# A second output projection inside the experts' stage behind it, and one recurrence ahead of the last group's slots

## The chip, the cores and the metric

One Trainium2 chip, one of its cores. The time is that of one execution on the device, in microseconds (us), median of the runs. Lower is better.

## The reference

Four different layers follow each other on 4 batches of 1024 tokens with 128 features, each of the form x = x + s * silu(f), s from a token mixer and f from a feed-forward part, both on the layer-normed x. Only parts of the second and the third layer matter here, given in outline. `layernorm` without scale stands for `_layernorm`.

```python
# layer 1: attention, 16 heads of 8; its output projection
attn = jax.nn.softmax(energy, axis=-1) / sqrt(E)
out = jnp.einsum('bihv,bvhd->bihd', attn, v).reshape(B, N, E)
s = out @ W_out + b_out
# layer 1: feed-forward, each token through 2 of 8 experts
f = sum over the 2 chosen of  w * (gelu(xn @ W1[e] + b1[e]) @ W2[e] + b2[e])
f = layernorm(f) * gamma + beta
x = x + s * silu(f);  xn = layernorm(x)
# layer 2: a linear recurrence of complex powers A, written there with an FFT
y = real(ifft(fft(xn) * fft(C * A^t * B))) + D * xn
# layer 2: feed-forward, 2 of 8 experts with room for 640 tokens each
```

## The kernel before

Every stage is a `Stage` (L28): tensors of its own, semaphores, one block with a program for each engine, and at its end a barrier of all engines. SyncE issues nearly all loads and stores, in the order in which its program has them; GpSimd issues the sends of rows to places given by an index. All arithmetic is in f32 here. TOK is 4096, in 32 tiles of 128 tokens or 8 chunks of 512.

- `narrow_attention_stage` (L625) leaves in memory the unnormalised output `o1` [128 features, 4096] and the sums of the softmax `sums1` [16 heads, 4096]. Beside it the tokens' rows are sent to `sorted_x`, sorted by expert.
- `divided_projection` (L1206), a stage named "out": SyncE loads the sums as [128, 512] (L1224), the weights, the bias, and half of o in pieces (L1228). VectorE inverts the sums (L1265), SyncE stores the inverse (L1230), waits for it, and loads it spread over each head's 8 rows in eight chunks (L1234), with the rest of o between (L1236). VectorE divides a chunk (L1257), TensorE projects its four tiles into one of four banks (L1246), VectorE adds the bias and writes `s` (L1261).
- `sorted_experts_stage` (L1790), named "experts", runs 72 tiles of 128 sorted rows, four to a turn. For tile n: SyncE loads its rows (L1836, L1841) once tile n-4 is turned and its index kept; TensorE turns it (L1878, bank `xt`) and multiplies by its expert's first matrix (L1885, `up`), VectorE adds the bias (`add_bias`, L1955), ScalarE takes the gelu (L1934), TensorE turns the result (L1892) and multiplies it by the second matrix (L1901, `down`), VectorE adds that bias (`finish`, L1960), GpSimd weighs the rows (L1852) and sends them back to their tokens (L1855). TensorE's body for n is: turn n+2, up of n+1, turn the hidden rows of n, down of n-1. The first four bodies and the last four are written out, the rest is a loop (`iterations`, from L1822).
- `combine_and_send_stage` (L2393), named "mix1": for four groups of 8 tiles, sum of the two experts' rows, norm, gate, x, norm of x, turning into `xnT`, router scores (`score_group`, L2562), ranking, slots (`place_group`, L2590 to 2615), and GpSimd's 16 sends a group (L2498). VectorE's program runs them in an order written by hand, the scores and slots of group g-1 inside group g, and ends with `score_group(3)`, `rank_group(3)`, `place_group(3)` and then four recurrences `recur(b)` (L2617 to 2642), one per batch, each 8 instructions of 1024 columns. TensorE turns each result (L2700) and ScalarE copies it to `s` (L2760). The next stage is the experts' of layer 2.

Two lines set the ends that matter below:

```python
for b in range(BATCH):
    recur(b)                       # L2667, at VectorE's end
...
with eng.Fori(1, NL - 1) as j:     # L1825, the experts' loop
```

## Time and profile before

| | |
|---|---|
| median of 3 runs | 3506.58 us (3506.2 to 3508.32) |
| the profiled execution | 3507.76 us |
| its span, first to last instruction | 3506.0 us |
| TensorE busy, share of the span | 2860.7 us, 82% |
| VectorE | 2360.2 us, 67% |
| ScalarE | 1848.7 us, 53% |
| GpSimd | 1519.4 us, 43% |
| mean granted TensorE clock | 0.911 |
| transfers | 189.53 MB, mean 54 GB/s |

The shares are means over fifteen stages with different limits, so they are to be read stage by stage: the second output projection from 2592.3 to 2618.8, the experts of layer 1 from 2618.8 to 2841.7, mix1 from 2841.7 to 3029.8. In a timeline row stand the start in us from the span's start, the length, the engine (PE is TensorE, DVE VectorE, ACT ScalarE, POOL GpSimd, SPq SyncE's queue), the line, what is written and read, and in brackets the idle time before it with what ended it.

### The profile page before, as it was taken

What the parts mean: (1) busy time and instruction counts of PE and PEld (TensorE: products, weight loads), DVE (VectorE), ACT (ScalarE), POOL (GpSimd) and SP (SyncE); (2) the same over time, 40 slices, a digit from 0 to 9 for tenths busy, and PEclk for the clock granted to TensorE, in tenths of its full rate; (3) what the DMA queues carried; (4) which work ended last, traced back from release to release, by engine and by line L of the source; (5) the groups of instructions that cost most, each with busy time, mean ns of one, the idle gap of its engine ahead of it and who ended that gap; (6) DMA issues with size and microseconds to landing.
All of it is one profiled execution on the core that took longest, in us unless ns stands there. A gap on an engine that the chain in (4) does not pass through costs nothing. (4 is left out here: it accounts for less than half of the span.)

```text
span 3506.0 us, 66844 instructions
## 1 busy us (share of the span) xinstructions
PE 2860.7 (82%) x21143; PEld 1282.3 (37%) x21144; DVE 2360.2 (67%) x3457; ACT 1848.7 (53%) x2993; POOL 1519.4 (43%) x1115
## 2 busy tenths in 40 slices
PE   3999999999999996499965599999969932484994
PEld 1333333333333335433333122222226622362772
DVE  5666666666666655788886799999933346634663
ACT  2555555555555550144464399999954443244442
POOL 0889998999899991100000001101106625360000
PEclk9999999999999997799986699999989965696995
DMA  2011111111111114400003222222221150014001
GB/s 85 30 42 47 42 54 41 47 50 46 42 47 55 42 39 156 148 1 1 0 2 128 62 54 53 57 51 53 54 80 44 45 190 29 25 42 98 11 13 54
DMA packets 264612, 189.53 MB, mean 54 GB/s; under 512 B 148254, under 2 KB 210070, under 8 KB 263552
## 3 DMA queue, kind: packets, MB, share of 16 engines
q1 hardware_dynamic: 256288, 174.05, 17.5%
q0 software_dynamic: 8224, 14.24, 1.3%
q8 instruction: 50, 0.82, 0.1%
q14 instruction: 50, 0.41, 0.0%
HBM read 105.21 MB, written 67.55 MB: 49 GB/s over the span
## 5 line engine op out<-in xcount | busy, mean ns | idle before, releaser
L331 POOL TENSOR_TENSOR attn_esum<-attn_esum,attn_prob 128x1024 f32<-128x1024 f32 x384 | 904.4, 2355 | 30.8 <-ACT attn_prob L482 7.4
L553 DVE TENSOR_REDUCE attn_half_max<-attn_peek 128x2 f32<-128x1024 f32 x512 | 627.1, 1225 | 399.3 <-PE attn_peek L382 395.5
L482 ACT ACTIVATE attn_prob<-attn_score 128x1024 f32<-128x1024 f32 x512 | 512.8, 1022 | 247.3 <-PE attn_score L365 247.3
L848 ACT ACTIVATE attn_prob<-attn_score 128x512 f32<-128x512 f32 x1024 | 556.3, 596 | 72.5 <-PE attn_score L798 58.4
L865 DVE TENSOR_REDUCE attn_half_max<-attn_peek 128x2 f32<-128x1024 f32 x512 | 583.5, 1214 | 11.1 <-PE attn_peek L784 11.1
L412 PE MATMUL attn_acc<-attn_prob,attn_v 128*64 128x512 f32 x2048 | 487.9, 597 | 0.1
L814 PE MATMUL attn_acc<-attn_prob,attn_v 128*32 128x256 f32 x4096 | 327.8, 392 | 12.0 <-ACT attn_out L840 10.6
L1780 POOL DMA_INDIRECT sorted_x<-attn_sent_rows,attn_send x64 | 62.7, 980 | 555.1 <-PE attn_score L798 555.1
L784 PE MATMUL attn_peek<-attn_ke,attn_qe 48*128 48x512 bf16 x1024 | 203.0, 393 | 46.4 <-DMA attn_ke<-k 31.7
L382 PE MATMUL attn_peek<-attn_hi 64*128 64x512 f16 x1024 | 200.1, 388 | 34.4 <-DVE attn_half_max L553 34.4
L798 PE MATMUL attn_score<-attn_qe,attn_ke 49*128 49x512 bf16 x1024 | 200.6, 389 | 8.1 <-ACT attn_prob L848 6.0
L331 POOL TENSOR_TENSOR attn_esum<-attn_prob 128x1024 f32<-128x1024 f32 x64 | 151.0, 2360 | 126.7 <-ACT attn_prob L482 126.7
L412 PEld LDWEIGHTS attn_acc<-attn_prob,attn_v 128*64 128x64 f32 x2048 | 130.8, 137 | 201.1 <-issue 156.4
L1584 PE MATMUL experts_up<-experts_x,experts_up_w 128*128 (+1 forms) x816 | 200.0, 381 | 1.4 <-DVE experts_down_w L1673 1.4
L367 PE MATMUL attn_score<-attn_hi 64*128 64x512 f16 x1024 | 195.0, 378 | 0.0
L367 PE MATMUL attn_score<-attn_hi,attn_lo 64*128 64x512 f16 x1024 | 195.0, 377 | 0.0
L367 PE MATMUL attn_score<-attn_lo,attn_hi 64*128 64x512 f16 x1024 | 195.0, 377 | 0.0
L365 PE MATMUL attn_score<-attn_shift,attn_sel 64*128 64x512 bf16 x1024 | 194.8, 377 | 0.0
L1955 DVE TENSOR_TENSOR experts_pre<-experts_up,experts_b 128x512 f32<-128x512 f32 x112 | 77.4, 691 | 147.0 <-PE experts_up L1885 147.0
L2052 POOL MEMSET proj_zero<- 128x2340 f32 x1 | 2.0, 2048 | 381.6 <-POOLq L41 381.6
L1650 ACT ACTIVATE experts_a<-experts_up 128x512 f32<-128x512 f32 x136 | 81.2, 597 | 159.1 <-PE experts_up L1584 156.1
L1940 ACT ACTIVATE experts_hidT<-experts_ht 128x512 f32<-128x512 f32 x112 | 66.9, 597 | 165.0 <-PE experts_ht L1892 165.0
(516 smaller groups left out, 4603.6 us busy)
## 6 DMA issues: line engine op xcount, KB each, us to landing
attn_xb<-attn_x_all SPq DMA_DIRECT2D x66, 256.0 KB, 2.5
attn_invB<-inv SPq DMA_DIRECT2D x64, 256.0 KB
o<-attn_out SPq DMA_DIRECT2D x32, 512.0 KB, 2.7
out_o<-o SPq DMA_DIRECT2D x8, 2048.0 KB
mix_f<-picked SPq DMA_DIRECT2D x16, 512.0 KB, 7.4
experts_x<-sorted_x SPq DMA_DIRECT2D x112, 65.0 KB
attn_qe<-q SPq DMA_DIRECT2D x192, 32.0 KB
attn_ke<-k SPq DMA_DIRECT2D x192, 32.0 KB
```

The costliest lines, as they stand in the source:

```text
L331: nc.gpsimd.tensor_tensor(own, before, prob[:, u % NPROB, :, :], ALU.add).then_inc(added, 1)
L367: last = mm(score[:, u % 2, h, :], ks[r, slot, WHICH["k"], keys], qs[r, slot, WHICH["q"], queries], start=(n == 0), stop=False)
L382: last = mm(peek[:, h, :], hi[r, slot, WHICH["q"], t * P:(t + 1) * P], hi[r, slot, WHICH["k"], half * CH:(half + 1) * CH], start=True, sto ...
L412: last = mm(acc[rows_of(h), :], v[:, slot, t, rows_of(h)], prob[:, u % NPROB, h, :], start=(t == 0), stop=(t == KT - 1))
L482: nc.scalar.activation(prob[:, u % NPROB, :, :], score[:, u % 2, :, :], ACT.Exp).then_inc(exped, 1)
L553: V.tensor_reduce(half_max[:, half, :, t], peek[:], AX.X, ALU.max, negate=True).then_inc(maxed, 1)
L784: last = mm(peek[:, m % NPEEK, n, :], qe[r, slot, pair, t * P:(t + 1) * P], ke[r, slot, pair, half * CH:(half + 1) * CH], start=True, stop ...
L798: last = mm(score[:, (PAIR * k + n) % RING, :], ke[r, slot, pair, t * P:(t + 1) * P], qe[r, slot, pair, c * CH:(c + 1) * CH], start=True, ...
L814: last = mm(acc[h * COL:(h + 1) * COL, cols], v[:, slot, t, h, :], prob[:, (HG * s + h) % NPROB, cols], start=(t == 0 and p == 0), stop=(t ...
L848: nc.scalar.activation(prob[:, n % NPROB, :], score[:, n % RING, :], ACT.Exp).then_inc(exped, 1)
L865: V.tensor_reduce(half_max[:, half, PAIR * pair:PAIR * (pair + 1), t], peek[:, m % NPEEK, :, :], AX.X, ALU.max, negate=True).then_inc(maxe ...
L1584: ins = nc.tensor.matmul(out, ws[pw][:, cols], xs[px][own], start=start and n == 0, stop=stop and n == 2)
```

## The change

1. The stage "out" is gone. What it did is a class `DividedProjection`, which `sorted_experts_stage` takes as `beside` for layer 1 (not for layer 2). Its loads stand in SyncE's queue behind those of the first four tiles; o comes in one load. The store of the inverse and its eight loads stand behind the load of tile 7. VectorE inverts and scales behind its first body, and divides one chunk behind each of the bodies 4 to 11.
2. For that, two more turns (bodies 4 to 11) are written out instead of being in the loop, on TensorE, VectorE and SyncE. Behind body 11 TensorE projects all 32 tiles in eight rounds of four into the two banks of `xt`, VectorE takes each round, and TensorE goes on when the last is taken.
3. In mix1 `recur(0)` stands ahead of the scores, ranks and slots of the last group; each recurrence waits for its own group's rows in `xnT` and the first no longer for all four.

```diff
-def divided_projection(nc, name, o_d, sums_d, inv_d, scale, w, bias, s):
...
 
-def sorted_experts_stage(nc, name, ident, blocks, xs_d, expert_d, weights, y_d):
+class DividedProjection:
+
+
+
+    AT = 4
+    ROUNDS = NT // AT
+
+    def __init__(self, st, nc, o_d, sums_d, inv_d, scale, w, bias, s):
+        self.nc, self.o_d, self.sums_d, self.inv_d, self.scale, self.w, self.bias, self.s = nc, o_d, sums_d, inv_d, scale, w, bias, s
+        self.heads = sums_d.shape[0]
+        assert TOK == P // self.heads * CH
+        self.o, self.inv, self.sums = st.sb("attn_o", [P, TOK]), st.sb("attn_inv", [P, NCH, CH]), st.sb("attn_sums", [P, CH])
+        self.wt, self.bias_b = st.sb("attn_wt", [P, D]), st.sb("attn_bias", [P, D])
+        self.w_in, self.sums_in, self.inv_out, self.o_in, self.inverted, self.scaled, self.divided, self.projected, self.summed = (
+            st.sem(n) for n in ("w_in", "sums_in", "inv_out", "o_in", "inverted", "scaled", "divided", "proj_done", "proj_summed"))
+        self.inv_in = [st.sem(f"inv_in{n}") for n in range(NCH)]
+
+    def pieces(self, a):
+        return a.rearrange("h (n t) -> (h n) t", n=P // self.heads)
+
+    def tiles(self, r):
+        return range(r * self.AT, (r + 1) * self.AT)
+
+    def load(self, sp):
+        sp.dma_start(self.sums[:], self.pieces(self.sums_d)).then_inc(self.sums_in, DMA)
+        sp.dma_start(self.wt[:], self.w).then_inc(self.w_in, DMA)
+        sp.dma_start(self.bias_b[:], broadcast_rows(self.bias)).then_inc(self.w_in, DMA)
+        sp.dma_start(self.o[:], self.o_d[:]).then_inc(self.o_in, DMA)
+
+    def spread(self, sp):
+        sp.wait_ge(self.inverted, 1)
+        sp.dma_start(self.pieces(self.inv_d), self.sums[:]).then_inc(self.inv_out, DMA)
+        sp.wait_ge(self.inv_out, DMA)
+        for i in range(NCH):
+            sp.dma_start(self.inv[:, i, :], self.inv_d[:, i * CH:(i + 1) * CH].unsqueeze(1).to_broadcast([self.heads, P // self.heads, CH])
+                         ).then_inc(self.inv_in[i], DMA)
+
+    def invert(self, dve):
+        V = self.nc.vector
+        dve.wait_ge(self.sums_in, DMA)
+        V.reciprocal(self.sums[:], self.sums[:]).then_inc(self.inverted, 1)
+        dve.wait_ge(self.w_in, 2 * DMA)
+        V.tensor_scalar(self.wt[:], self.wt[:], self.scale, None, ALU.mult).then_inc(self.scaled, 1)
+
+    def divide(self, dve, i):
+        dve.wait_ge(self.o_in, DMA)
+        dve.wait_ge(self.inv_in[i], DMA)
+        own = slice(i * CH, (i + 1) * CH)
+        self.nc.vector.tensor_tensor(self.o[:, own], self.o[:, own], self.inv[:, i, :], ALU.mult).then_inc(self.divided, 1)
+
+    def project(self, pe, bank, r):
+        if r == 0:
+            pe.wait_ge(self.scaled, 1)
+            pe.wait_ge(self.divided, NCH)
+        if r >= 2:
+            pe.wait_ge(self.summed, r - 1)
+        for n, t in enumerate(self.tiles(r)):
+            last = self.nc.tensor.matmul(bank[:, n * P:(n + 1) * P], self.o[:, t * P:(t + 1) * P], self.wt[:], start=True, stop=True)
+        last.then_inc(self.projected, 1)
+
+    def take(self, dve, bank, r):
+        dve.wait_ge(self.projected, r + 1)
+        own = self.tiles(r)
+        self.nc.vector.tensor_tensor(self.s[:, own[0]:own[-1] + 1, :], bank[:].rearrange("p (t d) -> p t d", d=D),
+                                     self.bias_b[:].unsqueeze(1).to_broadcast([P, len(own), D]), ALU.add).then_inc(self.summed, 1)
+
+
+def sorted_experts_stage(nc, name, ident, blocks, xs_d, expert_d, weights, y_d, beside=None):
...
         names = ("consts", "x_turned", "x_copied", "projected", "biased", "gelu_done", "h_turned", "h_copied", "summed", "y_ready")
         (consts, x_turned, x_copied, projected, biased, gelu_done, h_turned, h_copied, summed, y_ready) = (st.sem(n) for n in names)
         stored, kept, shared, loaded = st.sem("stored"), st.sem("kept"), st.sem("shared"), [st.sem(f"loaded{u}") for u in range(UNROLL)]
+        job = beside(st) if beside else None
         block = st.block()
         NCONST = 2
 
-        def iterations(eng, body):
+        def iterations(eng, body, between=None):
             for u in range(UNROLL):
                 body(u, u, True, False)
-            with eng.Fori(1, NL - 1) as j:
+            START = 3 if between else 1
+            for n in range(1, START):
+                for u in range(UNROLL):
+                    body(UNROLL * n + u, u, False, False)
+            if between:
+                between()
+            with eng.Fori(START, NL - 1) as j:
                 for u in range(UNROLL):
                     body(UNROLL * j + u, u, False, False)
             for u in range(UNROLL):
...
             sp.dma_start(b2[:], broadcast_rows(weights.weights_d[3].rearrange("e d -> (e d)"))).then_inc(consts, DMA)
             for n in range(UNROLL):
                 sp.dma_start(x[:, n, :], xs_d[n * P:(n + 1) * P, :]).then_inc(loaded[n], DMA)
-            with sp.Fori(1, NL) as l:
+            AHEAD = 3 if job else 1
+            if job:
+                job.load(sp)
+            for l in range(1, AHEAD):
+                for u in range(UNROLL):
+                    sp.wait_ge(x_turned, UNROLL * (l - 1) + u + 1)
+                    sp.wait_ge(kept, UNROLL * (l - 1) + u + 1)
+                    sp.dma_start(x[:, u, :], xs_d[(UNROLL * l + u) * P:(UNROLL * l + u + 1) * P, :]).then_inc(loaded[u], DMA)
+                if l == 1:
+                    job.spread(sp)
+            with sp.Fori(AHEAD, NL) as l:
                 for u in range(UNROLL):
                     sp.wait_ge(x_turned, UNROLL * (l - 1) + u + 1)
                     sp.wait_ge(kept, UNROLL * (l - 1) + u + 1)
...
             turn_x(0, 0, False)
             turn_x(1, 1, False)
             project(0, 0, False)
-            iterations(pe, body)
+
+            def attention():
+                pe.wait_ge(x_copied, 3 * UNROLL + 2)
+                for n in range(job.ROUNDS):
+                    job.project(pe, xt[:, n % 2, :], n)
+                pe.wait_ge(job.summed, job.ROUNDS)
+
+            iterations(pe, body, attention if job else None)
             down(blocks - 1, 1, True)
 
         @block.scalar
...
 
             dve.wait_ge(consts, NCONST * DMA)
             add_bias(0, 0, False)
-            iterations(dve, body)
+
+            def with_division(n, u, first, final):
+                body(n, u, first, final)
+                if isinstance(n, int) and n == 0:
+                    job.invert(dve)
+                elif isinstance(n, int) and 4 <= n < 4 + NCH:
+                    job.divide(dve, n - 4)
+
+            def attention():
+                for n in range(job.ROUNDS):
+                    job.take(dve, xt[:, n % 2, :], n)
+
+            if job:
+                iterations(dve, with_division, attention)
+            else:
+                iterations(dve, body)
             finish(blocks - 1, 1)
 
...
             def recur(b):
                 u = xnT[:, b * SEQ:(b + 1) * SEQ]
                 Er, Ei, Wr, Wi, decay = (kept[:, n, :] for n in range(KEPT))
+                dve.wait_ge(evacuated, b + 1)
                 if b == 0:
-                    dve.wait_ge(evacuated, NG)
                     dve.wait_ge(kept_in[0], DMA)
                 link(V.tensor_tensor(vr, Er, u, ALU.mult))
                 if b == 0:
...
                 second_factors(g)
                 if g:
                     place_group(g - 1)
+            recur(0)
             score_group(NG - 1)
             rank_group(NG - 1)
             place_group(NG - 1)
-            for b in range(BATCH):
+            for b in range(1, BATCH):
                 recur(b)
 
         @block.tensor
...
             weights = ExpertWeights(held, nc, "experts1", inputs("L1_ffn_", "W1 b1 W2 b2"))
             narrow_attention_stage(nc, ident, q1, k1, v1, o1, sums1, scratch("max1", [2, 2, 16, P], BF16),
                                    lambda st: RowScatter(st, s, send, pick_weight, sorted_x, weights, picked[1]))
-            divided_projection(nc, "out1", o1, sums1, scratch("inv1", [16, TOK]), D ** -0.5, a["L1_attn_W_out"], a["L1_attn_b_out"], s)
-            sorted_experts(1, BLOCKS, weights)
+            inv1 = scratch("inv1", [16, TOK])
+            sorted_experts(1, BLOCKS, weights, lambda st: DividedProjection(st, nc, o1, sums1, inv1, D ** -0.5, a["L1_attn_W_out"],
+                                                                            a["L1_attn_b_out"], s))
         ROOM = 5 * TOK // 4 // P
         with ExitStack() as held:
             weights = ExpertWeights(held, nc, "experts2", inputs("L2_ffn_", "w1 b1 w2 b2"))
```

SyncE, from the end of attention, before (`out_` is the projection's stage, `inv` and `o` lie in memory):

```order
L1224 DMA out_sums<-sums 128x512
L1225 DMA out_wt<-in_L_attn_W_out 128x128
L1226 DMA out_bias_b<-in_L_attn_b_out 128x128
L1228 DMA out_o<-o 128x512 x4
L1230 DMA inv<-out_sums 128x512
L1234 DMA out_inv<-inv 128x1x512 x5
L1236 DMA out_o<-o 128x512
L1234 DMA out_inv<-inv 128x1x512
L1236 DMA out_o<-o 128x512
L1234 DMA out_inv<-inv 128x1x512
L1236 DMA out_o<-o 128x512
L1234 DMA out_inv<-inv 128x1x512
```

and with the change (`attn_` in the experts' stage is the projection's):

```order
L1837 DMA experts_expert<-owner 1x72
L1838 DMA experts_b<-in_L_ffn_b 128x1024
L1840 DMA experts_x<-sorted_x 128x130 x4
L1744 DMA experts_attn_sums<-sums 128x512
L1745 DMA experts_attn_wt<-in_L_attn_W_out 128x128
L1746 DMA experts_attn_bias<-in_L_attn_b_out 128x128
L1747 DMA experts_attn_o<-o 128x4096
L1848 DMA experts_x<-sorted_x 128x130 x4
L1751 DMA inv<-experts_attn_sums 128x512
L1754 DMA experts_attn_inv<-inv 128x1x512 x8
L1848 DMA experts_x<-sorted_x 128x130 x4
```

The four tiles that stood behind a stage's end now stand ahead of the projection's loads, and tiles 4 to 7 and 8 to 11 behind its two bundles.

TensorE in the experts' stage, with the change, end of body 11 and the loop's first turn:

```order
L1915 MATMUL experts_out<-experts_w,experts_hidT 128x128
L1915 ISA
L1915 MATMUL experts_out<-experts_w,experts_hidT 128x128
L1777 MATMUL experts_xt<-experts_attn_wt,experts_attn_o 128x128 x32
L1829 UNCONDITIONAL_BRANCH
L1829 ISA
L1891 REGISTER_ALU
L1892 MATMUL experts_xt<-identity,experts_x 128x128
L1881 ISA
L1881 TENSOR_LOAD experts_expert
```

Before, the 32 products stood alone in their stage (L1246) and the loop began behind body 3.

VectorE in mix1, at the end of the third group's slots, before:

```order
L2614 TENSOR_TENSOR mix_each_pick<-mix_hot,mix_weight 128x128
L2615 TENSOR_REDUCE mix_sent_rows<-mix_each_pick 128x2x8
L2562 TENSOR_TENSOR mix_score<-mix_lg,mix_bias_b 128x64
L2563 TENSOR_REDUCE mix_red<-mix_score 128x8
L2564 TENSOR_TENSOR mix_shifted<-mix_score,mix_red 128x64
L2573 TENSOR_REDUCE mix_red<-mix_score 128x8
```

and with the change:

```order
L2650 TENSOR_TENSOR mix_each_pick<-mix_hot,mix_weight 128x128
L2651 TENSOR_REDUCE mix_sent_rows<-mix_each_pick 128x2x8
L2659 TENSOR_TENSOR mix_f<-mix_kept,xnT 128x1024
L2662 TENSOR_TENSOR mix_f<-mix_kept,xnT 128x1024
L2665 SCALAR_TENSOR_TENSOR mix_f<-mix_kept,mix_f 128x1024
L2666 SCALAR_TENSOR_TENSOR mix_f<-mix_kept,mix_f 128x1024
L2669 TENSOR_TENSOR mix_f<-mix_f,mix_kept 128x1024
L2672 TENSOR_TENSOR mix_f<-mix_f,mix_kept 128x1024
L2673 TENSOR_TENSOR mix_f<-mix_f 128x1024
L2678 SCALAR_TENSOR_TENSOR mix_f<-xnT,mix_dd,mix_f 128x1024
L2598 TENSOR_TENSOR mix_score<-mix_lg,mix_bias_b 128x64
L2599 TENSOR_REDUCE mix_red<-mix_score 128x8
```

Eight instructions of 1024 columns have moved ahead of the last group's scores; the other three recurrences stay at the end.

## Rows read from the trace of the kernel before

**Rows 1.** Windows by stage: engine busy us (count), TensorE clock, DMA share, GB/s.
```profile
2592.30:2618.80 26.50, 11.16 (x64) 10.24 (x64) 13.76 (x18) 0.00 (x0) 0.00 (x0) 0.65 0.65 184
2618.80:2841.70 222.90, 186.95 (x1080) 130.38 (x1080) 70.77 (x144) 94.19 (x218) 131.33 (x217) 0.97 0.16 43
2841.70:3029.80 188.10, 34.47 (x144) 30.21 (x144) 133.79 (x340) 59.54 (x104) 71.56 (x77) 0.50 0.31 99
```

**Rows 2.** Timeline of the second output projection: start us, us, engine, line [idle before].
```profile
2592.34 0.36 SPq L1224 DMA_DIRECT2D out_sums<-sums  x1
...
2595.02 3.35 DVE L1265 RECIPROCAL out_sums<-out_sums 128x512 f32<-128x512 f32 x1 [34.10 <-DMA out_sums<-sums]
2598.29 0.16 DVE L1267 TENSOR_SCALAR out_wt<-out_wt 128x128 f32<-128x128 f32 x1
2598.40 0.33 SPq L1230 DMA_DIRECT2D inv<-out_sums  x1
2600.64 3.18 SPq L1234 DMA_DIRECT2D out_inv<-inv  x5
...
2604.58 0.69 DVE L1257 TENSOR_TENSOR out_o<-out_o,out_inv 128x512 f32<-128x512 f32 x1 [6.12 <-DMA out_inv<-inv]
```

**Rows 3.** DMA view of window 2602.5 to 2613.5.
```profile
DMA packets 1615, 2.96 MB, mean 269 GB/s; under 512 B 175, under 2 KB 175, under 8 KB 1614
```

**Rows 4.** Timeline, first us of the experts' stage.
```profile
2618.78 0.25 SPq L1833 DMA_DIRECT2D experts_expert<-owner  x1
...
2628.58 0.69 DVE L1955 TENSOR_TENSOR experts_pre<-experts_up,experts_b 128x512 f32<-128x512 f32 x1 [1.06 <-PE experts_up L1885]
...
2630.52 0.69 DVE L1955 TENSOR_TENSOR experts_pre<-experts_up,experts_b 128x512 f32<-128x512 f32 x1 [1.25 <-PE experts_up L1885]
...
2631.85 0.27 PE L1878 MATMUL experts_xt<-identity,experts_x 128*128 128x128 f32 x1
```

**Rows 5.** Timeline of mix1 from the third group's slots to the next stage.
```profile
2948.16 0.29 DVE L2615 TENSOR_REDUCE mix_sent_rows<-mix_each_pick 128x16 f32<-128x128 f32 x1
...
2948.96 3.58 PE L2684 MATMUL mix_lg<-mix_wr,xnT 128*128 128x8 f32 x16 [1.11 <-ACT xnT L2735]
...
2962.96 0.23 DVE L2562 TENSOR_TENSOR mix_score<-mix_lg,mix_bias_b 128x64 f32<-128x64 f32 x1 [14.52 <-DMA o<-attn_out]
...
2976.73 1.21 DVE L2623 TENSOR_TENSOR mix_f<-mix_kept,xnT 128x1024 f32<-128x1024 f32 x1
...
2988.98 1.23 DVE L2623 TENSOR_TENSOR mix_f<-mix_kept,xnT 128x1024 f32<-128x1024 f32 x1
...
3001.11 0.98 POOL L2498 DMA_INDIRECT sorted_x<-mix_sent_rows,mix_send  x1 [0.30 <-issue]
...
3029.78 0.26 SPq L1833 DMA_DIRECT2D experts_expert<-owner  x1
```

**Rows 6.** Timeline, last loop tiles of the experts' stage, VectorE.
```profile
2819.52 0.69 DVE L1955 TENSOR_TENSOR experts_pre<-experts_up,experts_b 128x512 f32<-128x512 f32 x1 [0.98 <-PE experts_up L1885]
...
2820.85 0.29 DVE L1960 TENSOR_TENSOR experts_y<-experts_out,experts_b 128x128 f32<-128x128 f32 x1 [0.64 <-PE experts_out L1901]
...
2821.96 0.69 DVE L1955 TENSOR_TENSOR experts_pre<-experts_up,experts_b 128x512 f32<-128x512 f32 x1 [0.82 <-PE experts_up L1885]
```

**Rows 7.** Timeline, projection products at the lower and at the full clock.
```profile
2605.42 6.53 PE L1246 MATMUL out_acc<-out_wt,out_o 128*128 128x128 f32 x32 [18.22 <-DVE out_o L1257]
...
2614.85 2.36 PE L1246 MATMUL out_acc<-out_wt,out_o 128*128 128x128 f32 x16 [0.18 <-DVE out_o L1257]
```

**Rows 8.** Timeline, first and fifth of five up-projections, TensorE.
```profile
2629.25 1.12 PE L1885 MATMUL experts_up<-experts_w,experts_xT 128*128 x2 [0.25 <-issue]
...
2640.60 1.12 PE L1885 MATMUL experts_up<-experts_w,experts_xT 128*128 x2 [0.23 <-issue]
```

**Rows 9.** Windows of the experts' stage, split where the granted clock changes.
```profile
2621.30:2628.10 6.80, 4.15 (x7) 1.59 (x7) 0.69 (x1) 2.32 (x5) 0.73 (x4) 0.50 0.33 91
2628.10:2832.00 203.90, 182.80 (x1074) 128.79 (x1073) 70.08 (x143) 91.84 (x214) 129.56 (x211) 1.00 0.16 43
```

63 lines of the change are left out of this document (2 added, 61 removed).

## The prediction

> **What bounds the kernel now.** One core runs stage after stage with a barrier between them, so a microsecond counts only where it shortens the chain of its own stage. The busy shares of the page are means over such stages, and its chain of waits ends in the very last stage; neither says anything of the two places that change. I read the windows of the two stages, then their timelines in order of time, then the transfers.
>
> In the second output projection, window 2592.3 to 2618.8, TensorE works 11.2 us of 26.5 and ScalarE and GpSimd nothing [rows 1]. Its timeline is one chain [rows 2]: the sums' load is issued at 2592.34, VectorE inverts them at 2595.02 for 3.35 us, the inverse goes out to memory at 2598.40 and comes back spread over the heads from 2600.64 on, the first division stands at 2604.58. Behind it the loads of o and of the inverse run at 269 GB/s, full [rows 3]. The stage costs latency and transfer, not arithmetic. It ends where the experts' first load is issued, 2618.78 [rows 4].
>
> The experts' stage behind it, 222.9 us for 72 tiles, has TensorE busy 187 us and VectorE 71 us [rows 1]: TensorE sets its pace and VectorE has room. In mix1 (the combination, the routing and the recurrences) VectorE is the chain: 133.8 of 188.1 us busy. Its longest idle time there is 14.52 us, from 2948.45 to 2962.96, ahead of the last group's scores [rows 5]. The name beside that wait is a transfer of an early stage, which cannot be it. By the program VectorE waits for TensorE's score products, and these are shown from 2948.96 for 3.58 us, so over at 2952.54: 4.1 us of the wait are explained, 10.4 us are not. The runs of before lie within 2.1 us of each other, so I take those 10.4 us as present in all of them.
>
> **The change, part by part.** Times after a "+" count from the experts' first load, 2618.78 before.
>
> *The stage of its own goes.* From 2592.34 to 2618.78: -26.4 us. The barrier between attention and whatever follows stays.
>
> *The experts' first loads.* SyncE now issues sums, weights, bias and o between the first four tiles and tiles 4 to 7, and they share the transfers' bandwidth. In front of tile 4 lie 0.51 MB of biases, 0.26 of tiles, 0.39 of sums, weights and bias and 2.10 of o, 3.3 MB together; at 269 GB/s [rows 3] that is 12.2 us, from about +2: tile 4 lands near +15. It was turned at 2631.85, +13.1 [rows 4]: 2 us late. The Trainium skill (DMA: Bandwidth & Descriptors, section Queues, rings and completion order) says that each DMA engine consumes descriptors in the order of its ring, which is what would put tile 4 behind o; no row here shows the order, and without it tile 4 would be in time and the next term would stand alone.
>
> *VectorE's inversion*, 3.35 us, and the scaling of the weights, 0.16 [rows 2], stand between the second and the third addition of the up-projection's bias. These are at 2628.58 (0.69 long) and 2630.52 [rows 4], with 1.25 us between them: the third comes 2.3 us late, and the activation, TensorE's turning and the output behind it as well. This runs beside the late tile 4; the larger counts: +2.4 us. At the mean rate of the old stage, 184 GB/s [rows 1], tile 4 would land at +20 and this term be 7.
>
> *SyncE's queue.* Behind tile 7 it waits for the inverse (+14), stores it, waits for the landing (2.24 us between the two issues at 2598.40 and 2600.64 [rows 2]) and issues eight loads of 0.64 us (3.18 for five): free for tile 8 at +22. The 2.1 MB of the inverse take 7.8 us from +17, so tile 8 lands near +26; with a pace of 2.83 us tile 8 is wanted at +15.3 + 4 x 2.8 = +26.5. I take +0.3 us; between 0 and 4 by the slower rate.
>
> *Eight divisions*, 0.69 us each, one behind each of tiles 4 to 11. At the quickest pace seen VectorE's output addition ends at 2821.14 and the next bias addition begins at 2821.96 [rows 6]: 0.82 us, enough. Cost 0, cover: VectorE's wait for TensorE. Without it 8 x 0.69 = 5.5.
>
> *The projection itself* stops TensorE between tiles 11 and 12, and with it all who wait for it. Ahead: VectorE's last output addition and last division, 0.29 + 0.69, and two hand-overs, 1.2 us. Then eight rounds of four products: 16 rows (two rounds) took 2.36 us [rows 7], 1.18 a round, 9.4 together; VectorE's addition of 0.69 per round fits under it with two banks. Behind: the last addition and hand-overs, 0.9. Sum 11.5 us, against 10.0 if what ScalarE does meanwhile saves a bubble at the restart, and 15.2 at the lower clock, where 32 rows took 6.53 us (most of them at half clock), 1.63 a round [rows 7].
>
> *Eight bodies written out* in place of two turns of the loop. The first four, also written out, took 2640.60 - 2629.25 = 11.35 us from one up-projection to the fourth behind it [rows 8], the whole stage from 2628.1 to 2832.0 at 2.83 us a tile (203.9 us for 72, [rows 9]): no gain from straight code at this end of the stage, so 0. At the far end 2.44 us a tile are seen (2819.52 to 2821.96, [rows 6]); that would be 8 x 0.39 = -3.1. The Trainium skill (Runtime: NRT & Kernel Launch, section Instruction fetch mechanics) says that a taken branch breaks the sequential prefetch and straight code hides it; by that alone the sum would be 3.1 us lower, and the first four bodies speak against it here.
>
> *The first batch's recurrence ahead of the last group's slots.* One recurrence takes VectorE 2988.98 - 2976.73 = 12.25 us [rows 5]. It needs only the first two groups' rows (already turned) and buffers that are free by then. In its new place it fills 2948.45 to 2960.7 and the scores still start when the signal comes, 2962.96: -12.25 us at VectorE's end, which sets the stage's: only the last turning and its copy follow it, and the next stage begins at 3029.78 [rows 5]. Queued behind it: GpSimd's sends of the last group, which ended at 3002.1 [rows 5] and move by at most a microsecond or two, while VectorE will end near 3013. Bounds: -4.1 if the unexplained 10.4 us start anew behind the recurrence, -14.5 if they vanish.
>
> **Sum.** -26.4 + 2.4 + 0.3 + 11.5 = -12.2 for the projection, -12.25 for the recurrence: -24.5. The profiled execution took 3507.76 us, its span 3506.0; that gives 3483.3, and the median of the three runs lies 1.2 below the profiled one: **3482 us**. A measurement of this kernel can tell about 0.2%, 7 us, from no change.
>
> **Rivals.**
> 1. *Tiles starve.* The 4.2 MB of o and inverse share the way with tiles that come just in time. For: the arrival times above are late, or early by half a microsecond. Against: 269 GB/s held for 11 us. At 184 GB/s: + 4.5 + 2.5, **3489**. Chance 0.15.
> 2. *The late signal moves along.* If whatever holds TensorE's score signal for 10.4 us starts only where VectorE has nothing to do, it comes behind the recurrence and only 4.1 us are gained: **3490**. For: nothing explains it. Against: GpSimd's sends run beside it either way. 0.12.
> 3. *Better than the sum.* The signal comes at once (-2.3) and the written-out bodies keep the pace of the far end (-3.1): **3477**. For: both numbers stand in rows; against: the first four bodies. 0.18. The Trainium skill's rule on branches, cited above, is its second half.
> 4. *TensorE stays at the lower clock in the experts' stage.* At full clock it is the pace. The stage spends 2621.3 to 2628.1 at half clock after idle time of TensorE, then 204 us at full [rows 9]; the change makes the first 15 us of the stage thinner. If the clock fell for the stage, each tile would cost 1.63/1.18 of 2.83 us, 1.08 more, 72 x 1.08 = 78 us: **3560**. It decides from 24.5 / 1.08 = 23 tiles at half clock on. Against: after the old stage's longer idle time it rose 7 us into the work. 0.03. The Trainium skill (TensorE: Matmul & The Clock Gate, HAM oscillation) says that idle stretches of TensorE bring the lower clock back, which is the mechanism of this rival.
> 5. *The new chain does nothing for the end*: the gains of both parts are eaten by waits that I don't see. 3505; 0.02.
>
> **How the numbers follow.** The forecast, 3478 to 3487, has 0.50. Rivals 1 and 2 reach 3490, with the uncovered divisions 3496; rival 3 and the refill bubble reach 3474. Range 3473 to 3496; it leaves out rivals 4 and 5 and mixtures. Faster by over 0.2% (below 3499.6) are the forecast and rivals 1 to 3: 0.95. Rival 5: same, 0.02. Rival 4: slower, 0.03.
>
> **What would show it.** The experts' first load near 2592.3. The reciprocal right behind the second bias addition; the third near +14.1. The turning of tile 4 at +15, of tile 8 at +26.5, with a wait for a transfer under 1 us. The divisions without a shift of the next bias addition. A gap of 11.5 us in TensorE's expert work with 64 rows in it. The experts' stage 236 to 238 us long. In mix1 the first recurrence at once behind the third group's slots, then under 3 us of idle time, mix1 12 us shorter. Wrong would be: waits for tiles of 4 us and more (rival 1), a wait of 10 us behind the recurrence (rival 2), half clock beyond the first 10 us of the experts (rival 4).

## The result and the profile after

| | before | after |
|---|---|---|
| median | 3506.39 us (3503.86 to 3508.32, 4 runs) | 3478.78 us (3475.54 to 3481.29, 4 runs) |
| ratio, 95% interval | | 0.9921 (0.9904 to 0.9938) |
| profiled execution, its span | 3507.76, 3506.0 | 3476.27, 3474.6 |
| second output projection and experts' stage | 26.4 + 222.9 | 235.6 |
| mix1 | 188.1 | 172.6 |

The change takes 27.6 us off; 24.5 were forecast. Windows by stage of the kernel after, in the order of [rows 1] (TensorE, its weight loads, VectorE, ScalarE, GpSimd, then granted clock, DMA share, GB/s):

```profile
2590.90:2826.50 235.60, 196.67 (x1144) 139.05 (x1144) 84.25 (x162) 94.52 (x218) 131.63 (x217) 0.96 0.22 62
2826.50:2999.10 172.60, 34.23 (x144) 30.14 (x144) 133.94 (x340) 59.54 (x104) 73.69 (x77) 0.50 0.34 108
```

The first window is 12.7 us longer than its counterpart in [rows 1], and the window of 26.4 us ahead of it is gone: -13.7, where -12.2 was forecast. In mix1 VectorE has the same 340 instructions and the same 134 us of work, in 15.5 us less time; -12.25 was forecast. The two sum to -29.2, the profiled executions differ by 31.5; the rest lies in stages that the change doesn't touch (the experts' first load is issued 1.4 us earlier in the span than the old stage's was).

Timeline of the kernel after at the start of the experts' stage, whose first load is issued at 2590.91; the rows answer to [rows 4]:

```profile
2600.42 0.69 DVE L1976 TENSOR_TENSOR experts_pre<-experts_up,experts_b 128x512 f32<-128x512 f32 x1 [0.93 <-PE experts_up L1899]
...
2601.03 3.34 DVE L1760 RECIPROCAL experts_attn_sums<-experts_attn_sums 128x512 f32<-128x512 f32 x1
...
2604.36 0.68 DVE L1976 TENSOR_TENSOR experts_pre<-experts_up,experts_b 128x512 f32<-128x512 f32 x1
...
2605.72 0.33 PE L1892 MATMUL experts_xt<-identity,experts_x 128*128 128x128 f32 x1 [1.74 <-DMA experts_x<-sorted_x]
...
2606.57 2.01 PE L1899 MATMUL experts_up<-experts_w,experts_xT 128*128 x2 [0.52 <-ACT experts_xT L1948]
```

and the window of the clock's fall:

```profile
2606.70:2610.10 3.40, 3.40 (x11) 2.26 (x12) 0.69 (x1) 0.64 (x2) 1.24 (x2) 0.50 0.45 106
```

Tile 4 is turned at +14.8, as forecast (+15), and the third addition stands at +13.5 (forecast +14.1). What wasn't forecast is the last row: TensorE has just waited 1.74 us, its granted clock falls to 0.5 from 2606.7 to 2610.1, and the up-projection takes 2.01 us instead of 1.12. Tile 5 is turned at +19.6, 3.8 us later than before, not 2.4. By tile 13 only 2.1 of these are left (+40.56 against +38.44).

The same timeline at the insertion:

```profile
2634.51 0.68 DVE L1768 TENSOR_TENSOR experts_attn_o<-experts_attn_o,experts_attn_inv 128x512 f32<-128x512 f32 x1
2635.34 7.85 PE L1777 MATMUL experts_xt<-experts_attn_wt,experts_attn_o 128*128 128x128 f32 x64 [1.18 <-DVE experts_attn_o L1768]
2636.51 0.69 DVE L1783 TENSOR_TENSOR s<-experts_xt,experts_attn_bias 128x512 f32<-128x512 f32 x1 [1.31 <-PE experts_xt L1777]
...
2643.22 0.69 DVE L1783 TENSOR_TENSOR s<-experts_xt,experts_attn_bias 128x512 f32<-128x512 f32 x1 [0.20 <-PE experts_xt L1777]
2644.35 0.33 PE L1892 MATMUL experts_xt<-identity,experts_x 128*128 128x128 f32 x1 [1.16 <-DVE s L1783]
```

Lead 1.18 and end 1.16 us are near the forecast (1.2 and 0.9); the 64 rows take 7.85 us, 0.98 a round, not the 1.18 of [rows 7].

VectorE in mix1, from the third group's slots to the last group's scores and its slots, answering to [rows 5]:

```profile
2933.58 0.29 DVE L2651 TENSOR_REDUCE mix_sent_rows<-mix_each_pick 128x16 f32<-128x128 f32 x1
2933.78 1.21 DVE L2659 TENSOR_TENSOR mix_f<-mix_kept,xnT 128x1024 f32<-128x1024 f32 x1
...
2944.72 1.28 DVE L2678 SCALAR_TENSOR_TENSOR mix_f<-xnT,mix_dd,mix_f 128x1024 f32<-128x1024 f32 x1
2946.04 0.22 DVE L2598 TENSOR_TENSOR mix_score<-mix_lg,mix_bias_b 128x64 f32<-128x64 f32 x1
...
2952.94 0.28 DVE L2628 TENSOR_TENSOR_SCAN mix_upto<-mix_goes_on,mix_tally 128x64 f32<-128x64 f32 x1 [0.80 <-PE mix_tally L2728]
```

The 14.52 us of idle time are gone altogether, 2.3 more than the recurrence's 12.25. TensorE's score products ended at 2937.96 and their signal arrived at 2940.70, still 2.7 us late, but nobody waited for it. (This arrival is the semaphore's own record in the trace, which no row above shows; where VectorE waits, the start of the scores shows it too.)

### The profile page after: what moved, and what is told of

It is laid out like the page before. It is cut to its first block and busy times, and to the rows that moved or that the text cites. A ratio compares the mean times of both kernels' runs of the same rounds, so it can differ in the third digit from the quotient of the medians.

```text
span 3474.6 us, 66734 instructions
## 1 busy us (share of the span) xinstructions
PE 2857.3 (82%) x21143; PEld 1279.6 (37%) x21144; DVE 2359.7 (68%) x3457; ACT 1848.8 (53%) x2993; POOL 1521.8 (44%) x1115
## 3 DMA queue, kind: packets, MB, share of 16 engines
q1 hardware_dynamic: 255280, 174.05, 17.6%
## 5 line engine op out<-in xcount | busy, mean ns | idle before, releaser
L367 PE MATMUL attn_score<-attn_lo,attn_hi 64*128 64x512 f16 x1024 | 194.7, 377 | 0.0
L367 PE MATMUL attn_score<-attn_hi,attn_lo 64*128 64x512 f16 x1024 | 194.7, 377 | 0.0
L365 PE MATMUL attn_score<-attn_shift,attn_sel 64*128 64x512 bf16 x1024 | 194.7, 377 | 0.0
```

The source lines that it names most:

```text
L367: last = mm(score[:, u % 2, h, :], ks[r, slot, WHICH["k"], keys], qs[r, slot, WHICH["q"], queries], start=(n == 0), stop=False)
```

## The experiments

Each set of runs was made on one chip, with the kernel before run beside it there. The sets lie on different chips, and the kernel before had another median on nearly each: 3515.1, 3516.2, 3497.7 and 3497.8 us. So gains are compared within a set, and the lengths of stages are read from the profiles. A gain in us is worked out from the ratio; the difference of the two medians can be up to 3 us off it, since the sets are small.

### The parts, and what they cost

**The recurrence's move alone** (the kernel before, with `recur(0)` and its waits as in the diff of the change).

> Kernel before with the recurrence move alone. Theory: the two unexplained delays of TensorE's score signal (10.4 us in the kernel before, 2.7 us seen in the kernel after, hidden there) cost nothing once VectorE has work, so the routing stage gains the recurrence's 12.25 us, the rest of the idle time (14.5 - 12.25 = 2.3) and about 1.2 at the count behind it: 15.7 us, 3490.7. Rival (what the forecast said): the signal comes when it did, 12.25 us, 3494.2. Second rival: the delay starts anew behind the recurrence, 4.1 us, 3502.3. In the profile: no idle time of VectorE ahead of the last scores for the theory, 2.3 us for the first rival, 10 us for the second.

3495.57 us against 3515.05 (17 runs): ratio 0.9944 (0.9932 to 0.9956), 19.7 us. Mix1 takes 172.0 us, and VectorE has no idle time ahead of the last scores:

```profile
2963.24 1.28 DVE L2642 SCALAR_TENSOR_TENSOR mix_f<-xnT,mix_dd,mix_f 128x1024 f32<-128x1024 f32 x1
2964.56 0.22 DVE L2562 TENSOR_TENSOR mix_score<-mix_lg,mix_bias_b 128x64 f32<-128x64 f32 x1
```

Both rivals fall. The time is not the theory's 3490.7, which started from the first chip's 3506.4. The gain is 4 us above the theory's 15.7, just inside the interval (15.5 to 23.9 us); the runs below give a reason.

**The projection's part alone**, with the recurrences back at the end:

```diff
-            recur(0)
             score_group(NG - 1)
             rank_group(NG - 1)
             place_group(NG - 1)
-            for b in range(1, BATCH):
+            for b in range(BATCH):
                 recur(b)
```

> Kernel after with the recurrence put back behind the last group's slots. Theory: the projection's part gives the stage of its own (26.4) against 12.7 us more in the experts' stage: -13.7 from the two profiles, 3492.7; the forecast's sum for this part was -12.2, 3494.2. If the parts add up, this and the run with the recurrence alone together give 27.6. The wait of VectorE ahead of the last scores: 14.5 us if the late signal belongs to the program, another number if it belongs to one execution.

3500.61 us on the same chip: ratio 0.9960 (0.9947 to 0.9973), 14.1 us. The experts' stage is 236.3 us long: 13.0 us against the first profile, 14.1 against the run above on this chip, where the two stages take 27.4 and 223.0 us. The parts together give 33.8 on this chip, not 27.6. And mix1 takes 195.3 us, 7.2 more than before. Timeline around the last scores:

```profile
2957.51 0.98 POOL L2534 DMA_INDIRECT sorted_x<-mix_sent_rows,mix_send  x1 [0.30 <-issue]
2960.63 0.23 DVE L2598 TENSOR_TENSOR mix_score<-mix_lg,mix_bias_b 128x64 f32<-128x64 f32 x1 [23.19 <-DMA experts_attn_inv<-inv]
```

The wait is 23.19 us here, not 14.5. The products ended at 2941.53, so the signal is 19.1 us late. The transfer named as releaser is again no possible one; what can be read is the length. The send in the first row is the last of its group, and the signal comes 2.1 us behind its end.

**Without the 32 products and the eight additions.**

```diff
-            iterations(pe, body, attention if job else None)
+            iterations(pe, body, (lambda: None) if job else None)
...
-                iterations(dve, with_division, attention)
+                iterations(dve, with_division, lambda: None)
```

> Kernel after without the 32 products of the output projection and the eight additions that take them (their part of the result is left out; loads, inversion and divisions stay). Theory: the insertion costs what tile 14's turning moved less what the two other terms took, 10.3 us: 3468.5. Rival: the forecast's 11.5, 3467.3 (not to be told apart by the time alone, but by the turning of tile 14: +43.1 against +41.9). Second rival: ScalarE and VectorE use the pause and catch up, 5 us or less: 3474 or more.

3470.72 us. Tile 14 is turned 2.6 us behind tile 13; in the kernel after it was 12.9. The insertion costs 10.3 us, as the theory said. But the stage is only 7.1 us shorter (228.5) and the whole takes 3470.7 where the theory had 3468.5, since tile 13 is turned at +44.0, not +40.6:

```profile
2618.55 2.91 SPq L1848 DMA_DIRECT2D experts_x<-sorted_x  x2
2618.76 1.06 PE L1915 MATMUL experts_out<-experts_w,experts_hidT 128*128 x8
2623.60 0.33 PE L1892 MATMUL experts_xt<-identity,experts_x 128*128 128x128 f32 x1 [3.79 <-DMA experts_x<-sorted_x]
```

In this timeline (first load at 2594.22) tile 4 came with a wait of 0.86 us only and the clock did not fall behind it; TensorE wanted tile 8 at +25.6 and got it at +29.4. The kernel after, kept back at half clock behind tile 4, turned tile 8 at +27.3 without a wait. Tile 8 is where the forecast's first rival sat: it is a matter of 2 us, and here its wait, 3.79 us, is all but the 4 us that the rival named as its sign. Tile 5 is turned at +17.8 here, 2.0 us later than before; so nearly all of the way on to the kernel after's +19.6 is its half clock.

**Eight bodies written out, in the kernel before, and nothing else.**

```diff
+            for n in range(1, START):
+                for u in range(UNROLL):
+                    body(UNROLL * n + u, u, False, False)
-            with eng.Fori(1, NL - 1) as j:
+            with eng.Fori(START, NL - 1) as j:
```

> Kernel before with eight more bodies of the first experts' stage written out in place of two turns of the loop, nothing else. Theory: straight code runs a tile in 2.52 us against 2.83 in the loop, 8 x 0.31 = 2.5 us: 3503.9. Rival (the forecast): no difference, 3506.4; the 2.52 us of the kernel after would then come from something else there. In the profile: the distance of the up-projections of tiles 4 to 11. The routing stage is that of the kernel before: VectorE's wait ahead of the last scores is 14.5 us again if the late signal belongs to the program.

Ratio 0.9990 (0.9981 to 0.9999), 3.5 us; the experts' stage 220.85 us against 222.89. TensorE's up-projections, first of the kernel before (loop), then of this one:

```profile
2646.15 1.12 PE L1885 MATMUL experts_up<-experts_w,experts_xT 128*128 x2
2649.38 1.12 PE L1885 MATMUL experts_up<-experts_w,experts_xT 128*128 x2 [0.67 <-ACT experts_xT L1927]
2652.07 1.12 PE L1885 MATMUL experts_up<-experts_w,experts_xT 128*128 x2
```

```profile
2643.58 1.12 PE L1893 MATMUL experts_up<-experts_w,experts_xT 128*128 x2
2645.99 1.12 PE L1893 MATMUL experts_up<-experts_w,experts_xT 128*128 x2
2648.60 1.12 PE L1893 MATMUL experts_up<-experts_w,experts_xT 128*128 x2
```

In the loop the distance from one tile to the next is 3.2 us once in each turn, just behind the branch; in the part that is written out none is above 2.8 us. Two turns gave 2.0 us. Mix1 takes 193.4 us and VectorE's wait 21.7: the late signal again, 17.6 us behind the products' end at 2948.32:

```profile
2965.94 0.23 DVE L2570 TENSOR_TENSOR mix_score<-mix_lg,mix_bias_b 128x64 f32<-128x64 f32 x1 [21.72 <-DMA o<-attn_out]
```

### The late signal

**GpSimd's sends held back** (the kernel before):

```diff
                 pool.wait_ge(maps_ready, g + 1)
+                if g == NG - 2:
+                    pool.wait_ge(logits, NG)
```

> Kernel before, and GpSimd begins the third group's sends only when TensorE's score signal of the last group is there (it can hold them, since the last group's sends begin 8 us later than these end). In three profiles without the recurrence move this signal came 10.4, 17.6 and 19.1 us after the end of the last score product, while GpSimd sent without a pause. Theory: these sends hold the signal; without them it comes within 0.1 us, VectorE's wait falls to about 4.1 us, and the routing stage takes 188.1 - 10.4 = about 178 us, 10 to 17 us less than before. Rival: the sends have nothing to do with it (TensorE's own last product is reported late when it has nothing behind it): the wait stays at 14 to 23 us, the time that of before.

3500.21 us against 3516.23: ratio 0.9955 (0.9940 to 0.9970), 15.8 us, from one wait of GpSimd. Mix1 takes 176.5 us. Timeline; the products start at 2952.20 and end at 2955.78:

```profile
2952.20 3.58 PE L2686 MATMUL mix_lg<-mix_wr,xnT 128*128 128x8 f32 x16 [1.11 <-issue]
...
2955.82 0.23 DVE L2564 TENSOR_TENSOR mix_score<-mix_lg,mix_bias_b 128x64 f32<-128x64 f32 x1 [4.13 <-PE mix_lg L2686]
...
2956.63 0.98 POOL L2500 DMA_INDIRECT sorted_x<-mix_sent_rows,mix_send  x1 [4.87 <-issue]
```

The scores begin 0.04 us behind the last product, and the releaser is now named rightly. The sends begin behind it.

**The score products done twice**, on the same chip:

```diff
                 last.then_inc(logits, 1)
...
+                if g == NG - 1:
+                    for t in range(GT):
+                        mm(lg[:, 1 - g % 2, t * E:(t + 1) * E], xnT[:, (g * GT + t) * P:(g * GT + t + 1) * P], wr[:], start=True, stop=True)
```

> Kernel before, and TensorE does the last group's eight score products a second time, into the other bank, behind the signal. Theory (sends hold the signal): no change, VectorE's wait 14 to 23 us. Rival (a last product is reported late because nothing follows it on TensorE): the products behind it push it out, the wait falls to about 4.1 us and the routing stage to about 178 us.

Ratio 1.0001 (0.9991 to 1.0010). VectorE's wait is 22.50 us. TensorE goes on at once, and still the signal of the first 16 rows comes 18.4 us late:

```profile
2947.14 3.58 PE L2684 MATMUL mix_lg<-mix_wr,xnT 128*128 128x8 f32 x16 [1.11 <-issue]
2950.57 3.56 PE L2690 MATMUL mix_lg<-mix_wr,xnT 128*128 128x8 f32 x16
```

```profile
2969.12 0.23 DVE L2562 TENSOR_TENSOR mix_score<-mix_lg,mix_bias_b 128x64 f32<-128x64 f32 x1 [22.50 <-DMA o<-attn_out]
```

**The kernel after once more**, on another chip.

> The kernel after itself, unchanged, beside many runs of the kernel before. In the runs made so far with other kernels the kernel before had a median of 3515 to 3516 us, not 3506, and the late score signal took 17 to 19 us in three profiles against 10.4 in the first. Theory: the signal's lateness differs from execution to execution and the kernel after is rid of it, so its own time stays (3476 to 3481) while its gain is larger than the 27.6 us first measured: 35 us, ratio about 0.990. Rival: the whole chip was slower by 10 us in those runs, the ratio is 0.992 again and the kernel after takes about 3488.

3481.04 us against 3497.68: ratio 0.9960 (0.9946 to 0.9973), 14.0 us. The theory's first half holds: the kernel after takes its 3480 on this chip too (in the profile the score signal is 0.01 us behind the products). Its second half and the rival fall: the gain is not larger but half as large (the medians alone differ by 16.6), because the kernel before is faster here. That led to the last run.

**The kernel before once more**, on a further chip.

> The kernel before itself, profiled once more. Its median was 3506.4, 3515.1, 3516.2 and 3497.7 us in four sets of runs, on as many chips, while the kernel after took 3478.8 and 3481.0. Theory: the sets differ by the lateness of the score signal alone: the first profile has 3507.8 us with 10.4, so the whole is 3497.4 plus the lateness, within 3 us, in this profile too, whatever the chip; the routing stage is 177.7 us plus the lateness. Rival: the chips differ by their general pace: the lateness is 10.4 again and other stages (the experts' 222.9 us, the part behind it 476.3) take the difference.

The profiled execution took 3498.39 us. Timeline around the last scores:

```profile
2952.70 3.58 PE L2684 MATMUL mix_lg<-mix_wr,xnT 128*128 128x8 f32 x16 [1.11 <-ACT xnT L2735]
...
2956.32 0.22 DVE L2562 TENSOR_TENSOR mix_score<-mix_lg,mix_bias_b 128x64 f32<-128x64 f32 x1 [4.12 <-PE mix_lg L2684]
```

No lateness at all, with the same instructions and 16 sends beside them, and a time of 3497.4 + 0, within 1 us: the theory. The medians bear it out: 3515.1, 3516.2 and the first chip's 3506.4, less the 17.6, 18.4 and 10.4 us read there, give 3497.5, 3497.8 and 3496.0. For a single execution it holds less well: of two other profiles close to the kernel before, products twice (3512.6 us) less its lateness gives 3494.2, and bodies written out (3507.4 us) gives 3489.8 where some 3495 were to be expected, so other stages differ by 3 to 6 us as well. In one table:

| profile | score signal late by | mix1 | mix1 less lateness |
|---|---|---|---|
| before, first chip | 10.4 us | 188.1 | 177.7 |
| projection's part alone | 19.1 | 195.3 | 176.2 |
| bodies written out | 17.6 | 193.4 | 175.8 |
| products twice | 18.4 | 194.7 | 176.3 |
| sends held back | 0.0 | 176.5 | 176.5 |
| before, last chip | 0.0 | 176.3 | 176.3 |
| recurrence's move alone | 3.0, hidden | 172.0 | |
| after; after once more | 2.7, hidden; 0.0 | 172.6; 172.3 | |

The signal's lateness goes by the chip, as far as one or two profiles of each can tell: on the three chips where it is late without the move, five profiles with the move have it 2.7 to 3.0 us late; on the chip of the kernel after's second set three profiles with the move have 0.0. There the kernel before has no profile; its median, 3497.7 us, is that of the last chip. Without the move mix1 takes 176 us plus the lateness (the first row's other 1.6 us are a second late signal, behind its count), and with it 171.9 to 173.1 in eight profiles, whatever the chip. The move is worth 4 us by itself and all the lateness that a chip has. With the 13 to 14 us of the projection's part that makes 17 to 18 us on a chip without lateness; 14.0 were measured there, with an interval of 9.4 to 18.9.

### What is to be had beyond the change

**Another order of loads**: o behind tiles 4 to 7, tiles 8 and 9 between the inverse's store and its spread (the kernel after).

```diff
     def load(self, sp):
...
-        sp.dma_start(self.o[:], self.o_d[:]).then_inc(self.o_in, DMA)
-    def spread(self, sp):
+    def spread(self, sp, tile):
+        sp.dma_start(self.o[:], self.o_d[:]).then_inc(self.o_in, DMA)
...
+        tile(2, 0)
+        tile(2, 1)
         sp.wait_ge(self.inv_out, DMA)
```

> Kernel after with SyncE's loads in another order: o goes behind tiles 4 to 7 instead of ahead of them, and tiles 8 and 9 are issued between the inverse's store and its spread. Theory: tile 4 is turned at +13.1 again, not +14.8, TensorE does not fall to half clock behind it, and tile 8 is in time: 1.5 to 3 us less than the kernel after in the experts' stage (232.6 to 234), whole 0.1% less. Rival: o and the inverse come later, VectorE waits for a division and the insertion begins later: equal or slower.

3480.05 us, the experts' stage 236.5 us (0.9 more than after, with a fall to half clock for 3.4 us behind the insertion): no gain, though tile 4 is turned at +13.4 and tile 8 at +24.7, as the theory said. The rival's wait is there:

```profile
2622.28 0.69 DVE L1770 TENSOR_TENSOR experts_attn_o<-experts_attn_o,experts_attn_inv 128x512 f32<-128x512 f32 x1 [2.04 <-DMA experts_attn_inv<-inv]
```

Tile 13 is turned at +40.3, where the kernel after has it at +40.6. The 2 us only changed places.

**All bodies written out**, of both experts' stages and with SyncE's loads likewise, once with that order of loads and once with the order of the kernel after:

```diff
-            with eng.Fori(START, NL - 1) as j:
+            for n in range(1, NL - 1):
+                if n == 3 and between:
+                    between()
                 for u in range(UNROLL):
-                    body(UNROLL * j + u, u, False, False)
+                    body(UNROLL * n + u, u, False, False)
```

> The same order of loads, and every body of both experts' stages written out instead of a loop. Theory: the loop costs 0.3 us a tile (2.82 in the loop against 2.52 written out); 56 tiles of the first and 32 of the second stage are in the loop, 17 + 9.6 us, so some 26 us less than the run with the order of loads alone, about 3450. Rival: the 2.52 us hold only near the stage's start, where GpSimd's sends are not yet dense, and the pace of the later tiles is set elsewhere: no gain beyond 3 us. Second rival: so long a straight program starves the engines of instructions: slower.

> Kernel after with every body of both experts' stages written out, the loads in the order of the kernel after. Theory: straight code is all of the gain of the run with everything written out (14.3 us in the first, 7.4 in the second experts' stage), the order of the loads none of it: the experts' stages 221 to 223 us and 7 us shorter, the whole 21 us below the kernel after, about 3458. Rival: tile 8 is missed by 2 to 4 us as in the run without the products, 3461.

3459.01 us (ratio 0.9836, 0.9822 to 0.9849, against 3516.23) and 3458.42 us (0.9892, 0.9877 to 0.9907, against 3497.68). Each lies 21 to 23 us below the run of its own set that still has the loop (3480.05 and 3481.04). The first experts' stage takes 222.2 and 223.4 us, 12.3 to 14.3 less, the part behind mix1 6.5 to 7.4 less. Windows of 100 us inside the first experts' stage, of the kernel after and of the first of these runs:

```profile
2690.00:2790.00 100.00, 90.57 (x528) 63.47 (x529) 34.65 (x71) 45.10 (x107) 64.79 (x108) 1.00 0.17 46
```

```profile
2690.00:2790.00 100.00, 98.71 (x580) 69.46 (x579) 37.98 (x78) 49.20 (x116) 69.84 (x117) 1.00 0.19 51
```

TensorE goes from 91 to 99% busy: 580 rows against 528. At 15 rows a tile that is 2.59 us a tile instead of 2.84. In this stretch the stage is now bound by TensorE's work alone; its start and the insertion are not.

**Divisions and insertion later**, in the run with everything written out and the other order of loads: `n - 6` in place of `n - 4` in `with_division`, `n == 4` in place of `n == 3` above, and TensorE's wait for `x_copied` ahead of the insertion four tiles later.

> The run with everything written out and the other order of loads, and now the divisions stand behind tiles 6 to 13 instead of 4 to 11 and the insertion four tiles later. In that run VectorE waited 2.0 us for the first piece of the inverse, and the tiles 8 to 10 took 4.4 and 3.5 us instead of 2.6. Theory: the wait goes, the tiles up to the insertion keep 2.6 us, the first experts' stage is 2 to 3 us shorter (219 to 220), 3456. Rival: what is late next is a tile's load behind the eight pieces of the inverse; the same 222.

3457.09 us, the first experts' stage 221.9: the rival. VectorE's wait for the inverse is gone, and tile 10, whose load stands behind the eight pieces of the inverse, is late by 2.68 us instead. All three versions with everything written out are equal within what can be told.

## Why the prediction was right, and where it was not

- **The stage of its own, -26.4**: right for the first profile. In the five others that have the stage it took 26.7 to 28.9 us, so this term is good to some 2.5 us only.
- **The late tile 4, +2.4**: the mechanism was right, and tile 4 came at +14.8. The term was too small: behind the wait of 1.74 us the granted clock was at the lower level for 3.4 us, and tile 5 was 3.8 us late. The forecast had weighed the lower clock for the whole stage (rival 4) and not for one wait.
- **SyncE's queue, +0.3**: right in the kernel after, but by luck of 2 us. The load of tile 8 was issued at +21.9 as forecast (+22), but landed near +29.4 and not +26 in the run without the products; tile 8 waited for it there, and the kernel after was slow enough not to.
- **Eight divisions, 0**: right; none moved a bias addition.
- **The insertion, +11.5**: 10.3, since a round took 0.98 us and not the 1.18 of [rows 7]; the second of the rounds there had begun only when VectorE's division was done.
- **Written-out bodies, 0**: this step was wrong. "The first four bodies speak against it" read the wrong rows: the distance in [rows 8] ends in the loop already, three of its five up-projections (tiles 2, 3 and 4) are written out and two are not. Two turns written out gave 2.0 us, two thirds of rival 3's second half. The runs with everything written out give 0.25 us a tile, 1 us a turn of four tiles. The Trainium skill (Runtime: NRT & Kernel Launch, section Instruction fetch mechanics) has straight code faster because a taken branch breaks the sequential prefetch; the traces agree with the direction. They do not show the prefetch apart from the rest that a loop needs, its register arithmetic above all.
- **Sum of the projection's part**: +3.8, +10.3 and -1.7 (written-out bodies) give 12.4 where 12.7 were measured and 14.2 forecast. Three sizes were off, in both directions.
- **The recurrence, -12.25**: 15.5 in the profiles. The step that failed is "the scores still start when the signal comes", with a signal fixed at 14.5 us behind VectorE's last work. The delay isn't a fixed time: it was gone when GpSimd's sends were held back, and with VectorE at work 2.7 to 3.0 us of it were left. And "I take those 10.4 us as present in all of them" held for the first set of runs only: on the last chip it was 0, on another its time says the same, and on two it was 17.6 to 19.1. Of the gain in the first set 4 us are the plain wait filled, the rest the lateness. So that the whole gain came near the forecast is luck of the chip: on one without lateness the same change gave 14.0 us, and on one with more of it its two parts gave 33.8, where 24.5 were forecast. The time of the kernel after, 3479 to 3481 us, does not depend on it.
- **The rivals.** Rival 1 (tiles starve) did not come in the kernel after: tile 4 came when forecast and tile 8 was in time; the 1.4 us beyond the forecast behind tile 4 are the lower clock's. Rival 2 (the late signal moves along) is refuted: the scores follow the recurrence at once in each profile with the move. Rival 3 came true in both halves (3.2 where it had 2.3 us, though the signal did not come at once but was late out of sight; 2.0 where it had 3.1); the time of 3478.8 lies between its 3477 and the forecast's 3482. Rival 4 showed itself for 3.4 us only; its price for a tile at the lower clock, 1.63/1.18 = 1.38 times as long, was too low, since the same up-projection took 2.01 us there against 1.12. In the profiles the two parts gained 29.2 us, 4.7 more than forecast: a tile that was later than forecast (+1.1) stood against three terms that turned out better (insertion 1.2, written-out bodies 1.7, recurrence 3.2). The medians' 27.6 lie nearer.

## What to carry to other kernels

When a wait in a profile ends for no reason that the profile shows, take its length as a property of that execution and chip, not of the program: here it ran from 0 to 19 us over five profiles of the same wait, and a whole chip's median moved with it. Independent work put into such a wait makes the kernel both faster and steadier from chip to chip. It is worth what the wait is: 12.25 us of recurrence were worth 15.5 and 19.7 us where the signal was late, and mix1's 176.3 and 172.3 us make it worth 4 where it isn't. A stage bound by TensorE with small tiles should be written out before anything is inserted into it: the loop cost more than the whole insertion, and an order of loads that mends one late transfer is worth nothing until the next one in the queue is counted too.

## What was not expected of the hardware

- TensorE's signal behind the last group's products came 10.4 to 19.1 us after their end on three chips, and at once on a fourth, with the same instructions. Holding GpSimd's 16 back-to-back indirect sends (one every 1.29 us) until the signal was there left no lateness on the chip where the run with the products twice had 18.4 us; more work behind the products on TensorE did nothing. So on that chip these sends are needed for the delay. In the three profiles with 17.6 us and more the signal came only when the last of these sends was over, 0.7 to 2.1 us behind its end; in the first, with 10.4, it came 6.8 us ahead of that. How the sends bring it about is not shown, nor why the second and third groups' signals came at once (within 0.02 us) although sends ran beside them too, nor why the chips differ.
- With VectorE in its recurrence the sends themselves stretch from 0.98 to 1.93 and 2.02 us, and the signal arrived at 2940.70, inside the second of the long ones:

```profile
2936.16 0.98 POOL L2534 DMA_INDIRECT sorted_x<-mix_sent_rows,mix_send  x1 [0.30 <-issue]
2937.44 1.93 POOL L2534 DMA_INDIRECT sorted_x<-mix_sent_rows,mix_send  x1 [0.30 <-issue]
2939.67 2.02 POOL L2534 DMA_INDIRECT sorted_x<-mix_sent_rows,mix_send  x1 [0.31 <-issue]
```

 In this timeline of the kernel after VectorE's two scans of 2.29 us run from 2936.29 to 2940.90, so the signal came 0.2 us ahead of their end. In the four other profiles with the move and a late signal it came within 0.2 us of the second scan's end as well, each time inside the second long send. What lets it through then is open: no run changes the scans or the spacing of the sends by itself.
- A wait of 1.74 us of TensorE, 4 us after its clock had risen (2599.8), was followed by 3.4 us at the lower level (1.2 GHz). The same fall of 3.4 us is seen in the run without the products behind tile 8's wait of 3.79 us. Behind the insertion, with waits of 1.2 us on either side of it, it is there in the projection's part alone and in the other order of loads, and not in the kernel after.
